# Moving a small router from the next pair's attention into the seam behind it, in a one-core fused patch, attention, MLP and mixture-of-experts kernel

## The reference

```
h = silu(patches @ tok_W1 + b1) @ tok_W2 + b2;  h = concat([h, txt])
x = layernorm(h);  xn = rms_norm(x, ln1_w);  q, k, v = xn @ Wq, xn @ Wk, xn @ Wv   # q, k normalised by head
y = softmax((q k^T + bias) * scale, causal) @ v @ Wo + x
h = h + relu(rms_norm(y, ln2_w) @ W1) @ W2 + y
xt = layernorm(h);  scores = softmax(xt @ Wr)             # the router, Wr: 256 x 8
G, idx = top_k(scores.T, k)                               # k rows for each expert, over all rows
h = h + scatter_add(idx, G * (gelu(xt[idx] @ fW1 + fb1) @ fW2 + fb2))
```

## Time and profile before

| | us |
|---|---|
| median of 3 runs | 4518.1 (4512.38 to 4521.21) |
| profiled execution | 4522.34, its span 4520.5 |
| TensorE busy | 3966.2 (88%) |
| VectorE, ScalarE, GpSimd busy | 2400.7, 2034.7, 1716.0 |
| mean ScalarE exponential, VectorE mask product | 0.742, 0.869 |

### The profile page before, as it was taken

How to read it: one execution, slowest core, us unless ns; L and a number is a source line. 1 busy time by engine, 2 the same in 40 slices (tenths; PEclk the granted TensorE clock), 3 DMA queues, 4 the chain that set the end, 5 groups by cost and what they waited for, 6 DMA issues and landing times. The chain is left out here.

```text
span 4520.5 us, 76799 instructions
## 1 busy us (share of the span) xinstructions
PE 3966.2 (88%) x26370; PEld 2347.5 (52%) x26370; DVE 2400.7 (53%) x4843; ACT 2034.7 (45%) x3373; POOL 1716.0 (38%) x1366
## 2 busy tenths in 40 slices
PE   2699999999899899999989989726999999999998
PEld 1455555555555555555555555414555555555554
DVE  3455555555555555555545555366555555555554
ACT  0344444444444444444434444223555655565654
POOL 1132223323222232332223232103766666666666
PEclk8799999999999999999999999857999999999999
DMA  7422212222221222222122120071333233333233
GB/s 114 76 38 37 47 32 41 42 36 38 35 47 34 40 43 33 38 35 47 34 40 47 30 43 15 17 190 42 56 51 64 46 63 64 47 63 63 46 46 46
DMA packets 302872, 222.26 MB, mean 49 GB/s; under 512 B 111524, under 2 KB 290182, under 8 KB 302710
## 3 DMA queue, kind: packets, MB, share of 16 engines
q1 hardware_dynamic: 183550, 157.86, 18.2%
q0 software_dynamic: 107264, 62.29, 8.9%
q10 hardware_dynamic: 11896, 0.05, 0.2%
HBM read 117.43 MB, written 63.57 MB: 40 GB/s over the span
## 5 line engine op out<-in xcount | busy, mean ns | idle before, releaser
L1395 DVE TENSOR_TENSOR pr<-pr,bias_t 114x684 f32<-114x684 f32 x512 | 439.0, 869 | 235.5 <-ACT pr L1027 231.0
L1574 DVE SCALAR_TENSOR_TENSOR hTs<-hTe,scales,hTs 128x456 f16<-128x456 f32 x514 | 322.6, 687 | 446.6 <-ACT hTs L1141 446.6
L505 PE MATMUL G<-w2m,hT 128*114 128x256 f32 x2048 | 521.9, 391 | 42.0 <-ACT hT L1066 22.2
L1744 POOL DMA_INDIRECT out_dram<-contrib,idx_cur x256 | 515.5, 2014 | 103.8 <-issue 77.4
L1027 ACT ACTIVATE pr<-SC 114x684 f32<-114x684 f32 x512 | 376.2, 742 | 368.5 <-PE SC L442 368.2
L900 PE MATMUL SC<-xgT,ws 128*128 128x456 f16 x2316 | 469.7, 358 | 0.0
L1737 POOL DMA_INDIRECT xg<-xn_rows,idx_cur x264 | 419.4, 1589 | 117.1 <-issue 60.0
L490 PE MATMUL G<-yT,w1m 128*128 128x456 f32 x1024 | 412.3, 551 | 10.5 <-ACT yT L973 10.5
L505 PEld LDWEIGHTS G<-w2m,hT 128*114 128x114 f32 x2048 | 338.0, 178 | 126.3 <-ACT hT L1066 43.4
L370 PE MATMUL G<-img,w1t 128*128 128x392 f32 x768 | 311.6, 523 | 51.0 <-DMA b2t<-in_L_tok_b_dram 50.1
L1675 POOL TENSOR_TENSOR rstd<-mv,ln_eps 114x4 f32<-114x4 f32 x32 | 7.0, 218 | 906.0 <-DVE mv L1264 906.0
(11 more groups left out here) (230 smaller groups left out, 6928.0 us busy)
## 6 DMA issues: line engine op xcount, KB each, us to landing
raw<-in_x_dram SPq DMA_DIRECT2D x192, 196.0 KB, 6.2
img<-turned SPq DMA_DIRECT2D x384, 98.0 KB, 2.8
we<-in_L_ffn_W_dram SPq DMA_DIRECT2D x34, 1024.0 KB, 7.6
out_dram<-hy SPq DMA_DIRECT2D x32, 456.0 KB
xn_rows<-xn SPq DMA_DIRECT2D x32, 456.0 KB
xg<-xn_rows,idx_cur POOLq DMA_INDIRECT x264, 3.8
out_dram<-contrib,idx_cur POOLq DMA_INDIRECT x256, 5.4
bias_by_distance<-pr SPq DMA_DIRECT2D x1, 3241.9 KB, 37.4
```

The lines of the kernel that those rows point to most:

```text
L505: last = pe.matmul(part.g("w2", b)[0:T, at:at + D], hT[:, m, t * T:(t + 1) * T], w2m[:, m, :], start=m == 0, stop=m == MC - 1)
L1395: dve.tensor_tensor(pr[g % 4][:, :, :], pr[g % 4][:, :, :], bias_t[:, 2 * pair:2 * pair + 2, :], ALU.mult).then_inc(probs_done, 1)
L1574: dve.scalar_tensor_tensor(hTs[:, 1, m, :], hTe[:, m, :], scale_at(scales, 2, e), hTs[:, 0, m, :], ALU.mult, ALU.subtract).then_inc(h_spli ...
L1744: pool.indirect_dma_start(out=out_rows, out_offset=bass.IndirectOffsetOnAxis(ap=idx_cur[k4][:, t:t + 1], axis=0), in_=contrib[k][:, t, :], ...
```

## The change

The router's blocks leave the table of slots and the banks G. For pair i - 2 they now run in iteration i's seam, in SC1, which no score needs there: `pe_x2T` behind the second `pe_tok2`, `pe_rtT` behind `pe_yT`, `pe_rt` behind `pe_wo`. ScalarE copies x2T ahead of yT, VectorE copies logitsT ahead of its sum into y2 (`tail`) and the logits behind it. In the first iteration there is no pair i - 2: it runs on zeros (xn2 is cleared at the start) into an extra block of logits. In the last part two routers run, one in the seam and one at the end. Four semaphores of its own count the steps. The first piece of w2 now waits for the relu blocks 0 and 1, and pieces 1, 2 and 3 for two blocks each, where piece 0 waited for blocks 6 and 7. The ninth piece of w2 moves from slot 3 to slot 4. The patch steps of m = 0 move from slots 11, 12, 13, 16, 18, 19 to 11, 12, 13, 15, 16, 18, and those of m = 1 from two each in 28, 29, 30 to one each in 22, 24, 26, 27, 29, 30.

```diff
-        logits = sb("logits", [T, NTILES, NE])
+        logits_all = sb("logits", [T, NT + NTILES, NE])
+        logits = logits_all[:, NT:, :]
...
-            "router": [("x2T", 0), ("x2T", 1), ("rtT", 0), ("rt", 0)],
...
+            if g == 1 and not first:
+                pe.wait_ge(router_copied, 2 * j)
...
                 if n == 0:
-                    for m in range(MC - 2, MC):
+                    for m in range(2):
+                        part.wait_evacuated(pe, "w1", m)
+                if n in (1, 2, 3):
+                    for m in range(2 * n, 2 * n + 2):
                         part.wait_evacuated(pe, "w1", m)
...
-        for n, slot in enumerate((0, 1, 3, 4, 5, 6, 7, 8, 9, 10)):
+        for n, slot in enumerate((0, 1, 4, 4, 5, 6, 7, 8, 9, 10)):
             SLOTS[slot].append(("w2", range(6 + n, 7 + n)))
-        for slot, work in ((17, ("yq", 0)), (20, ("yq", 1)), (21, ("x2T", 0)), (22, ("x2T", 1)), (23, ("rtT", 0)),
-                           (24, ("rtT", 1)), (26, ("rt", 0))):
+        for slot, work in ((17, ("yq", 0)), (20, ("yq", 1))):
             SLOTS[slot].append(work)
-        for m, steps in ((0, {11: 1, 12: 1, 13: 1, 16: 1, 18: 1, 19: 1}), (1, {28: 2, 29: 2, 30: 2})):
+        for m, steps in ((0, {11: 1, 12: 1, 13: 1, 15: 1, 16: 1, 18: 1}), (1, {22: 1, 24: 1, 26: 1, 27: 1, 29: 1, 30: 1})):
...
+        def pe_x2T(j):
+            pe.wait_ge(xn2_done, j + 2)
+            for c in range(KC):
+                for t in range(NT):
+                    last = pe.transpose(SC[1][:, c, t * T:(t + 1) * T], xn2[:, t, c * 128:(c + 1) * 128], ident[0:T, 0:T])
+                last.then_inc(x2_turned, 1)
+
+        def pe_rtT(j):
+
+            for c in range(KC):
+                wait_standing(pe, x2_copied, KC * (j + 1) + (c + 1))
+                last = pe.matmul(SC[1][0:NE, 0, 0:W], wr[:, c, :], xsT[:, c, :], start=c == 0, stop=c == KC - 1)
+            last.then_inc(router_made, 1)
+
+        def pe_rt(j):
+            wait_standing(pe, router_copied, 2 * (j + 1) + 1)
...
                 pe_tok2(part, i, 1)
+                pe_x2T(i - 2)
                 pe_yT(part, i - 1)
+                pe_rtT(i - 2)
                 pe_wo(part, i - 1)
+                pe_rt(i - 2)
                 pe_y2T(part, i - 1)
...
-                    if not first and g == 12:
-                        for c in range(KC):
-                            x2_transposed(part, c)
...
+            def x2_transposed(j):
+                for c in range(KC):
+                    wait_standing(act, x2_turned, KC * (j + 1) + (c + 1))
+                    act.copy(xsT[:, c, :], SC[1][:, c, 0:W]).then_inc(x2_copied, 1)
...
             def iteration(part, i):
+                x2_transposed(i - 2)
                 yT_evacuate(part)
...
             def iteration(part, i):
                 front_a(part, i, False)
+                router_transposed(i - 2)
                 tail(part, i - 1)
+                router_out(i - 2)
                 front_b(part, i)
...
+            pool.memset(xn2[:, :, :], 0.0)
```

More of the change, by code:

```diff
@@ L261, in early_fusion_kernel @@
         ln2_stats, xn2_done = sem("ln2_stats"), sem("xn2_done")
+        x2_turned, x2_copied, router_made, router_copied = (
+            sem("x2_turned"), sem("x2_copied"), sem("router_made"), sem("router_copied"))
         h1_stored, xn2_stored = sem("h1_stored"), sem("xn2_stored")
@@ L306, in early_fusion_kernel @@
                       [("tok1", 1), ("tok2", 1)] + BANKED["front"][1] + BANKED["qkv"][1] + BANKED["qkT"] + [("next", 0)]),
-            "body": (body[0] + BANKED["turn"] + BANKED["router"] + [("next", 1)], body[1] + [("next", 0)]),
-            "final": (body[0] + BANKED["turn"] + BANKED["router"], body[1]),
-            "last": (BANKED["after"][0] + w1_blocks(0, 0, MC) + [("w2", 0), ("w2", 1)] + BANKED["router"],
+            "body": (body[0] + BANKED["turn"] + [("next", 1)], body[1] + [("next", 0)]),
+            "final": (body[0] + BANKED["turn"], body[1]),
+            "last": (BANKED["after"][0] + w1_blocks(0, 0, MC) + [("w2", 0), ("w2", 1)],
                      BANKED["after"][1] + w1_blocks(1, 0, MC)),
@@ L531, in pe_slot @@
                     pe_turn(part, j, work[1])
[L532 to L540, removed]
+                elif work[0] == "w2" and part.kind != "first":
+                    pe_w2(part, work[1])
         def pe_attention(part, j):
@@ L585, in pe_y2T @@
                 pe_transposes(part, ("y2T", c), lambda t: y2[:, t, c * 128:(c + 1) * 128])
[L587 to L606, removed]
+        def pe_x2T(j):
[11 more added lines that the diff above has]
+            wait_standing(pe, router_copied, 2 * (j + 1) + 1)
             for t in range(NT):
-                last = pe.transpose(part.g("rt", 0)[0:T, t * NE:(t + 1) * NE], logitsT[:, t * T:(t + 1) * T],
+                last = pe.transpose(SC[1][0:T, 1, t * NE:(t + 1) * NE], logitsT[:, t * T:(t + 1) * T],
                                     ident[0:NE, 0:NE])
-            pe_block(part, ("rt", 0), last)
+            last.then_inc(router_made, 1)
         RING = [G[0], G[1], SC[0][:, 0, :], SC[0][:, 1, :], SC[1][:, 0, :], SC[1][:, 1, :], Y[1]]
@@ L833, in _ @@
                 pe_turn(part, PAIRS - 1, t)
+            pe_x2T(PAIRS - 2)
             pe_yT(part, PAIRS - 1)
+            pe_rtT(PAIRS - 2)
             pe_wo(part, PAIRS - 1)
+            pe_rt(PAIRS - 2)
             pe_y2T(part, PAIRS - 1)
@@ L839, in _ @@
             pe_w2(part, range(16))
-            for c in range(KC):
[L841 to L844, removed]
+            pe.wait_ge(router_copied, 2 * PAIRS)
+            pe_x2T(PAIRS - 1)
+            pe_rtT(PAIRS - 1)
+            pe_rt(PAIRS - 1)
             pe.wait_ge(score_ready, 2)
@@ L1070, in yT_evacuate @@
                     act_evacuate(part, ("yT", c), yT[:, c, :])
-            def x2_transposed(part, c):
-                act_evacuate(part, ("x2T", c), xsT[:, c, :])
+            def x2_transposed(j):
+                for c in range(KC):
+                    wait_standing(act, x2_turned, KC * (j + 1) + (c + 1))
+                    act.copy(xsT[:, c, :], SC[1][:, c, 0:W]).then_inc(x2_copied, 1)
             act.wait_ge(consts_in, 16 * (6 + NE + KC))
@@ L1104, in _ @@
             part = Part("last", PAIRS)
+            x2_transposed(PAIRS - 2)
             yT_evacuate(part)
@@ L1108, in _ @@
             relu(part, range(4))
-            for c in range(KC):
-                x2_transposed(part, c)
+            x2_transposed(PAIRS - 1)
             act.wait_ge(shifted, 1)
@@ L1369, in mlp_stats, with router_transposed, router_out @@
                 stats(hy, mv2, ln2_stats)
[L1371 to L1379, removed]
+            def router_transposed(j):
+                wait_standing(dve, router_made, 2 * (j + 1) + 1)
+                dve.tensor_copy(logitsT, SC[1][0:NE, 0, 0:W]).then_inc(router_copied, 1)
+            def router_out(j):
+                wait_standing(dve, router_made, 2 * (j + 1) + 2)
+                at = NT * (j + 1)
+                dst = logits_all[:, at:at + NT, :] if isinstance(j, int) else logits_all[:, bass.ds(at, NT), :]
+                dve.tensor_copy(dst, SC[1][0:T, 1, 0:NT * NE].rearrange("p (t e) -> p t e", e=NE)).then_inc(router_copied, 1)
             def tail(part, j):
@@ L1406, in masked_probs @@
                         mlp_stats(part)
[L1407 to L1410, removed]
             part = Part("first", 0)
@@ L1434, in _ @@
                 normalise_turned(j, half)
+            router_transposed(j - 1)
             tail(part, j)
+            router_out(j - 1)
             relu(part, range(4, MC))
@@ L1439, in _ @@
             mlp_stats(part)
-            router_transposed(part)
-            router_out(part, j)
-            part.wait_evacuated(dve, "rt", 0)
+            router_transposed(j)
+            router_out(j)
+            dve.wait_ge(router_copied, 2 * (PAIRS + 1))
             dve.wait_ge(h1_stored, 16 * (PAIRS + 1))
```

## The result

The changed kernel took 4303.95 us (4302.83 to 4305.97, 4 runs), the kernel before 4519.66 us. The ratio is 0.9536 (0.9517 to 0.9554), 216 us less. The forecast was 4326 us, between 4298 and 4400.

A forecast was written before the change was run, and what follows sets the result against it. TensorE's own work plus its in-order queue's waits bound the kernel. Attention -165.5, seam +33.6 and clock -60 us, in all -192, took 4522.3 to 4330.6 us; from the 4518.1 us median, 4326 us, 8 in 10 between 4298 and 4400.

The forecast's parts named there:

- Late attention: From the second yq transposes (T) to the next seam: 14.62 us shrinks to 10.06, -4.56 us an iteration.
- The wait in slot 22: Late attention: TensorE newly waits for VectorE to read bank G0, 0.85 us, or 0.55 if VectorE is already free.
- That value products don't wait: Late attention: the -4.56 us holds only if value products don't wait for their probabilities.
- my cover: Late attention: patch steps behind the last scores leave 3.4 us for group 15's exponential and a 0.87 us mask product.
- The spreading itself costs: Late attention: the six patch steps take 4.14 us as a lump and 4.99 us spread.
- Seam: Router moved into the seam: of about 3 us, +0.95 us an iteration shows and 2 us sink into three waits.
- +0.1: Seam: added register instructions and waits from each `wait_standing`, unpriced by any row, taken as +0.1 us an iteration.
- Slot 4: Ninth down-projection piece moved from slot 3: its 0.58 us wait goes, plus 0.2 us from pairing, -0.78 us an iteration.
- Product by product: First down-projection pieces start 0.71 us earlier, but one 1.10 us wait before qkp's transposes replaces two: gain 0.
- Clock: TensorE's clock no longer falls in the loop: 1.93 us an iteration, 31 times, -60 us.

The follow-up runs named there:

- the third piece: Changed kernel with a third down-projection piece before the first qkp transposes, patch step of slot 18 in slot 22 and that of 22 in 28: 4298.24 us.
- the router alone: Kernel before with only the router moved into the seam; down-projection waits, slot 3 and patch steps left as they were: 4444.73 us.
- the lump: Changed kernel with patch steps back where they were, those of m = 1 two each in slots 28, 29, 30: 4445.03 us.
- the bare wait in slot 20: Changed kernel with a wait of TensorE for xn2 in slot 20, ahead of the second yq transposes, and no other work: 4440.8 us.
- the router three slots later: Kernel before with its router still in attention but three slots later, m = 1 patch steps behind it in slots 30 and 31: 4452.52 us.

## Why the prediction was right, and where its sum was off

**Late attention**: -4.56 forecast, -4.88 from T to the seam, less 0.16 us ahead of T, where yq 1 waits for the reading of yq 0: -4.72. The wait in slot 22 came as named, 0.59 us and not 0.85, for that reason: T itself is later and VectorE has more time. That value products don't wait held, but my cover was mis-stated. I reckoned 3.4 us against a mask product of 0.87 and called the spreading a cost of 0.85 us. With GpSimd's copy beside them three products need 4.17 us. The spread steps, which I took for the weak part of this change, carry 141 of its 216 us: without them the copy, the wait behind it and the falling clock come to 4.5 us an iteration. The step that failed is "The spreading itself costs": with the copy out of the way it does, 0.46 us and not 0.85, but with the copy where it is the spreading saves 4.5 us. GpSimd's copy stood in no term of the sum. The steps were meant as cover, but for a product of 0.87 us; that the cover was also enough for products held up by the copy was luck.

**Seam**: +0.95 and +0.1 forecast, +0.81 measured. Where the router stands behind the waits it costs 2.21 us more; the forecast said 2 us sink into them. This part came as reasoned.

**Slot 4**: -0.78 forecast, 0.84 by the run that takes it back. **Product by product**: 0 forecast, and 0.07 us an iteration the other way by its run. The wait before the transposes of qkp is 1.42 us where the sum gave 1.10; 0.24 of that is work ahead of it that ends sooner, and the transposes start 0.08 us later after the MLP blocks than before.

**Clock**: 1.93 us an iteration forecast, all of it came. That the waits left would not let it fall was right for this order of work, but not for the reason given. The length of a wait does not decide it: an idle stretch of 1.24 to 1.27 us in slot 21 makes the clock fall in 4 of 30 iterations, the 1.42 us before qkp in none of 30. And the forecast leaned on the seam's waits of 0.84 and 0.77 us, which stood at a clock of 1.00 in one window; with the router behind them the same two, as long and around the same transposes, had a fall behind them in 3 of 30. That not one iteration of the changed kernel fell is measured; the argument for it was too weak, and luck was in it.

In sum an iteration lost 6.6 us (-4.72 + 0.81 - 0.84 + 0.07 - 1.93) and not 6.22, 11 us in 30 iterations. The rest lies outside the loop's body. Windows of the kernel before: the last pair, from its transposes of xs to the last router product, and all behind it (us, then busy time of TensorE, its weight load, VectorE, ScalarE and GpSimd, clock, DMA share, GB/s).

```profile
2812.79:2934.57 121.78, 96.82 (x613) 61.59 (x612) 45.14 (x97) 35.95 (x63) 19.83 (x20) 0.87 0.05 15
2934.57:4520.50 1585.93, 1411.77 (x8458) 798.88 (x8458) 884.83 (x1541) 869.57 (x1392) 952.24 (x586) 0.94 0.34 63
```

The same two windows of the changed kernel:

```profile
2615.47:2722.67 107.20, 89.23 (x614) 59.22 (x613) 44.99 (x97) 34.98 (x62) 21.84 (x20) 0.96 0.05 15
2722.67:4301.00 1578.33, 1411.40 (x8458) 801.54 (x8458) 885.31 (x1541) 868.68 (x1393) 934.02 (x586) 0.94 0.34 64
```

The last pair lost 14.6 us. It has no patch product to cover anything; before, its router waited 2.84 us for xn2 and its clock was lower (0.87, now 0.96). I had priced it like the others, 4.3 us and the clock, 6.2 together: 8 us too little. The experts behind it, which the change does not touch, took 7.6 us less. They also differ between experiments that change nothing there: from the end of the router's last transposes to the end of the program it is 1571.0 us in the shortest of the 14 profiles and 1590.7 in the longest, 1581.5 and 1573.9 in the kernel before and the changed one. So these 7.6 us lie inside that scatter and can't be called the change's. Two runs with nearly the iteration of the changed kernel (80.72 and 80.78 us) took 4311 us, and in their profiles most of the difference lies in that stretch. What moves it is open; no run was made for it.

## What to carry to other kernels

When a stall is removed, ask what the other engines did in its shadow. Here a GpSimd copy ran there for nothing; with the stall gone it lay beside VectorE's products, and most of the gain hung on work that happened to stand in exactly that place; moving the copy served as well. Moved work is cheapest where the busy engine waits anyway: the same 3 us cost 0.8 us between three waits and 3.0 behind them, at a full clock. And a wait that ends a chain of another engine is not shortened by starting sooner; put ready work into it (the third piece, 0.7 us).

## What the runs showed of the hardware

A VectorE product of two SBUF tensors took 3.50 us instead of 0.87 beside a GpSimd copy of 2.98 us, and 0.87 us beside GpSimd's making of xn2. TensorE's clock fell after the same wait (2.29 us) in some iterations and not in others; one fall cost 1.5 us (82.90 and 84.41, 81.44 and 82.95 us) or 1.7 (84.67 and 86.35, 83.00 and 84.69). And three kernels whose work differs settled at one length, 85.33 us an iteration: the router alone, the lump, and the bare wait in slot 20, which comes near it from its thirteenth iteration on (85.56, 85.49, 85.37 us and so forth). A fourth, the router three slots later, has iterations of two lengths, and 28 of them in a row have a mean of 85.33 us too. The first two differ by slot 3 and the relu wait, 0.8 us by other runs, and at clocks of 0.98 and 0.96 still take the same time. That the place of the fall adjusts itself to the iteration is my reading; no run was made to show it.
